# A Mamba and mixture-of-experts layer in a software pipeline: two groups of the D term as TensorE products with a diagonal, two C-weighted states through ScalarE and GpSimd, and the FFN's slots moved

## The reference, cut to what matters

```python
x = x + _layernorm(mamba(_layernorm(x)))
x = x + _layernorm(ffn(_layernorm(x)))
# mamba: 512 inner channels, 16 states, 4 taps
x_in, z = split(x @ W_in)
u = silu(causal_depthwise_conv(x_in) + conv_b)
dt_lr, B, C = split(u @ W_xproj)
delta = softplus(dt_lr @ W_dt + b_dt)
h_t = exp(delta_t * A) * h_(t-1) + (delta_t * u_t) * B_t      # for each of 16 states n
y_t = sum over n of C_t[n] * h_t[n]
y = (y + D_skip * u) * silu(z)                                # D_skip * u is the D term
out = y @ W_out
# ffn: shared silu(x@g)*(x@u)@d, and 8 experts weighted by the top 2 of softmax(x @ router)
```

## Time and profile before

| | before |
|---|---|
| time, median of 3 runs (range) | 2335.7 us (2333.97 to 2335.87) |
| the profiled execution's time | 2333.0 us |
| its span, first to last instruction | 2331.2 us |
| busy: DVE, PE, POOL, ACT | 2155.3, 2070.9, 1963.8, 1644.8 us |
| mean granted TensorE clock | 0.945 |

### The profile page before, as it was taken

The page is one execution under the profiler, slowest core; times in us unless marked ns, Lnnn a source line. Parts: engine busy times, 40 slices in busy tenths (PEclk is TensorE's granted clock), DMA queues, the critical chain, the costliest instruction groups (busy, mean ns, idle before and its releaser), DMA issues. The chain is left out here.

```text
span 2331.2 us, 30455 instructions
## 1 busy us (share of the span) xinstructions
PE 2070.9 (89%) x9280; PEld 1347.3 (58%) x9280; DVE 2155.3 (92%) x3056; ACT 1644.8 (71%) x2488; POOL 1963.8 (84%) x1625
## 2 busy tenths in 40 slices
PE   7678989999898999989899999998989989997978
PEld 4355665656566565655656566565656656565654
DVE  4999999999999999999999999999999999998950
ACT  5656877777777676777777777777768777775632
POOL 4677998989989898998989899898988989798844
PEclk8659999999999999999999999999999999998979
DMA  5111212211122121112211121121122111111201
GB/s 144 33 44 37 71 55 60 59 55 55 56 64 64 51 68 51 56 57 63 64 51 59 60 60 55 60 59 56 50 67 61 55 60 50 55 56 46 71 20 46
DMA packets 92995, 134.28 MB, mean 58 GB/s; under 512 B 12048, under 2 KB 43024, under 8 KB 92832
## 3 DMA queue, kind: packets, MB, share of 16 engines
q1 hardware_dynamic: 92832, 132.34, 18.4%
HBM read 123.13 MB, written 9.18 MB: 57 GB/s over the span
## 5 line engine op out<-in xcount | busy, mean ns | idle before, releaser
L836 DVE TENSOR_TENSOR_SCAN h<-d_a,carry,d_bu 128x512 f32<-128x512 f32 x1024 | 1261.1, 1267 | 47.0 <-ACT d_a L633 38.4
L1103 POOL TENSOR_TENSOR d_bu<-delta_u,b_rows 128x1024 f32<-128x1024 f32 x512 | 1202.2, 2359 | 4.4 <-issue 0.2
L633 ACT ACTIVATE d_a<-delta,a_neg 128x512 f32<-128x512 f32 x1024 | 699.6, 691 | 499.0 <-DVE h L836 493.9
L465 PE MATMUL ht<-ident,h 128*128 128x128 f32 x4096 | 607.3, 293 | 100.9 <-DVE y_t L846 94.3
L465 PEld LDWEIGHTS ht<-ident,h 128*128 128x128 f32 x4096 | 503.5, 150 | 333.6 <-issue 123.3
L846 DVE SCALAR_TENSOR_TENSOR y_t<-ht,c_t,y_t 128x512 f32<-128x512 f32 x896 | 621.5, 735 | 2.2 <-PE ht L465 1.5
L540 PE MATMUL ring<-x_t,w_gate_sb 128*128 128x512 f32 x640 | 327.8, 638 | 21.7 <-ACT delta L798 17.9
L567 PE MATMUL dn<-w_down_sb,up_hidden 128*128 128x256 f32 x1280 | 302.9, 379 | 1.7 <-POOL up_hidden L1166 1.7
L547 PE MATMUL ring<-x_t,w_up_sb 128*128 128x512 f32 x640 | 292.5, 600 | 11.9 <-ACT silu_gate L732 11.8
L1161 POOL TENSOR_TENSOR up_hidden<-silu_gate,up_hidden 128x512 f32<-128x512 f32 x160 | 204.3, 1277 | 110.8 <-ACT up_hidden L736 79.6
L567 PEld LDWEIGHTS dn<-w_down_sb,up_hidden 128*128 128x128 f32 x1280 | 236.0, 190 | 60.0 <-issue 31.8
(11 more groups left out here) (127 smaller groups left out, 2029.3 us busy)
## 6 DMA issues: line engine op xcount, KB each, us to landing
b_rows<-b_rows_hbm SPq DMA_DIRECT2D x256, 256.0 KB, 3.4
coef_rows<-coef_rows_hbm SPq DMA_DIRECT2D x128, 256.0 KB, 3.5
xa<-L_attn_x_in SPq DMA_DIRECT2D x16, 512.0 KB, 5.0
xr<-L_attn_x_in SPq DMA_DIRECT2D x16, 512.0 KB, 5.1
out<-xr SPq DMA_DIRECT2D x15, 512.0 KB, 2.9
w_in_sb<-L_attn_W_in_in SPq DMA_DIRECT2D x1, 1024.0 KB, 6.3
w_gate_sb<-L_ffn_experts_gate_in SPq DMA_DIRECT2D x2, 512.0 KB, 4.9
w_up_sb<-L_ffn_experts_up_in SPq DMA_DIRECT2D x2, 512.0 KB, 5.5
```

The lines of the kernel that those rows point to most:

```text
L465: last = nc.tensor.transpose(HT[q % HTS][:, j * P:(j + 1) * P], H[:, (NS * c + n) % HS, j, a * P:(a + 1) * P], IDN[:, :])
L633: nc.scalar.activation(DA[i % DAS][:, :], DL[:, r, j, :], ACT.Exp, scale=ANEG[:, j, n:n + 1]).then_inc(ex.sem, 1)
L836: nc.vector.tensor_tensor_scan(H[:, (NS * s + n) % HS, j, :], DA[(n * J + j) % DAS][:, :], BU[:, (2 * n + j // 2) % 4, j % 2, :], CARRY[:, ...
L1103: nc.gpsimd.tensor_tensor(BU[:, (2 * n + h) % 4, :, :], DU[:, 2 * h:2 * h + 2, :], BB[:, n % 2, :].unsqueeze(1).to_broadcast([P, 2, T]), A ...
```

## The change

1. **D term of groups 0 and 1.** Two 128x128 diagonals of D_skip (`DIAG`) are made once. At the end of slot 63 PE multiplies them with u (`skip_product`) into the ring banks, and `transpose_y` adds its transposes on top instead of starting the bank. DVE's `skip_u` of these groups becomes a plain copy by ACT in slot 3 (`copy_y`). Groups 2 and 3 stay on DVE in slot 5. Their transposes go from slot 4 to slot 3, ahead of `x_in` (0).
2. **Two pieces of y.** Pieces 14 and 15, which DVE added in slot 20, are written with their C by ACT in slot 20 into `UP` (`side_state`), and POOL adds both onto `y_t` in slot 22 (`side_sum`). DVE's next add on the same rows, piece 18 in slot 24, waits for it.
3. **Slots.** Pairs 1 to 4 come two slots earlier, both gates of pair 1 are in slot 20, delta comes two slots earlier, the statistics of xa are in slots 16, 16, 24, 24 (before: 16, 16, 26, 36) and its mean in 30 (42). `cf` and `ct` go to the dn banks, are copied in slot 20 itself, and `ct` comes from slot 48 to slot 20, ahead of the first down product.

```diff
-        yd, y_first, y_last, xt = stage("yd", J), stage("y_first", NT), stage("y_last", NT), stage("xt", KM)
+        yd_copy, diag = stage("yd_copy", 2), stage("diag", 0)
+        yd, y_first, y_last, xt = stage("yd", J - 2), stage("y_first", NT), stage("y_last", NT), stage("xt", KM)
...
-        YD_PE, YD_DVE, Y_GATE, OUT_PE = (1, 4), (3, 3, 5, 5), 4, (5, 5, 6, 6)
+        YD_PE, YD_ACT, YD_DVE, Y_GATE, OUT_PE = (1, 3), 3, {2: 5, 3: 5}, 4, (5, 5, 6, 6)
...
-        PAIR_AT = (12, 22, 32, 42, 50)
+        PAIR_AT = (12, 20, 30, 40, 48)
+        GATE_AT = (12, 13, 20, 20, 30, 31, 40, 41, 48, 49)
...
+                    if with_scan and t == SLOTS - 1:
+                        for j in range(2):
+                            skip_product(s, lo, r, j)
+
+            def skip_product(c, lo, r, j):
+
+                pe.wait_ge(diag.sem, 2)
+                pe.wait_ge(u_s.sem, u_s.at(c, j + 1))
+                pe.wait_ge(*ring_user_before(c + 1, lo + 1, "yd", j))
+                nc.tensor.matmul(yd_bank(j)[:, :], DIAG[:, j, :], U[:, r, j, :], start=True, stop=False,
+                                 skip_group_check=True)
...
                 pe.wait_ge(*added(s - 1, SLOTS - NT - 1))
-                if j < 2:
-                    pe.wait_ge(*ring_user_before(s, lo, "yd", j))
-                else:
+                if j >= 2:
                     pe.wait_ge(norm["y"].sem, norm["y"].at(s - 2))
+                    if exists(lo):
+                        pe.wait_ge(ct.sem, ct.at(s))
...
+            def side_state(c, r, q):
+
+                n, a = q // NT, q % NT
+                act.wait_ge(ht_full.sem, ht_full.at(c, q + 1))
+                act.wait_ge(hf.sem, hf.at(c - 1, up_used(1)))
+                act.wait_ge(y_sum.sem, y_sum.at(c - 1))
+                nc.scalar.activation(UP[:, q - SIDE_Q[0], :], HT[q % HTS][:, :], ACT.Copy,
+                                     scale=CT[:, r, a, n:n + 1]).then_inc(y_side.sem, 1)
...
+            def copy_y(c, j, prepared):
+
+                act.wait_ge(full["yd"].sem, full["yd"].at(c, j + 1))
+                act.wait_ge(conv_last.sem, conv_last.at(prepared))
+                act.wait_ge(o_full.sem, o_full.at(c - 1))
+                nc.scalar.activation(YD[:, j, :], yd_bank(j)[:, :], ACT.Copy).then_inc(yd_copy.sem, 1)
...
+            def side_sum(c):
+
+                a = SIDE_Q[0] % NT
+                pool.wait_ge(y_side.sem, y_side.at(c))
+                pool.wait_ge(*added(c, SIDE_Q[1] - NT))
+                nc.gpsimd.tensor_tensor(YT[:, a:a + 2, :], YT[:, a:a + 2, :],
+                                        UP[:, :, :], ALU.add).then_inc(y_sum.sem, 1)
```

More of the change, by code:

```diff
@@ L163, in mamba_moe_kernel @@
         shift = {w: stage(f"shift_{w}", n) for w, n in dict(xa=2, o=2, x1=2, y=2).items()}
+        y_side, y_sum = stage("y_side", 2), stage("y_sum", 1)
         stream, tail = stage("stream", 1), stage("tail", NT)
-        scan, add_c, carry = stage("scan", NS * J), stage("add_c", (NS - 2) * NT), stage("carry_s", NS)
+        scan, add_c, carry = stage("scan", NS * J), stage("add_c", (NS - 2) * NT - 2), stage("carry_s", NS)
         stats = {w: stage(f"stats_{w}_s", 2 * NT) for w in ("xa", "o", "x1", "y")}
@@ L217, in z_bank @@
             return DN[j] if j < 2 else ring_bank("z", j)
+        SIDE_Q = ADDS[SIDE_SLOT]
         def added(c, q):
@@ L553, in ffn_part @@
                     pe.wait_ge(rt.sem, rt.at(c))
-                    pe.wait_ge(*ring_user_before(s, lo, "cf", 0))
-                    bank = ring_bank("cf", 0)
+                    pe.wait_ge(x1t.sem, x1t.at(c))
+                    bank = DN[1]
                     for a in range(NT):
-                        last = nc.tensor.matmul(bank[0:E, a * P:(a + 1) * P], COEF[:, a, :],
-                                                IDN[:, :], start=True, stop=True)
+                        last = nc.tensor.transpose(bank[0:E, a * P:(a + 1) * P], COEF[:, a, :], IDN[:, :])
                     last.then_inc(full["cf"].sem, 1)
@@ L695, in body @@
                         first_state(s, r, t - NT - 1)
+                    if with_scan and t == SIDE_SLOT:
+                        for q in SIDE_Q:
+                            side_state(s, r, q)
                     if ffn and t == 1:
@@ L699, in body @@
                         normed_y(s - 2)
+                    if ffn and t == YD_ACT:
+                        for j in range(2):
+                            copy_y(s - 1, j, s if with_scan else s - 1)
                     if ffn:
@@ L803, in prep_part @@
                     nc.scalar.activation(CT[:, o, :, :].rearrange("p a n -> p (a n)"),
-                                         ring_bank("ct", 0)[:, 0:NT * NS], ACT.Copy).then_inc(ct.sem, 1)
+                                         CT_BANK, ACT.Copy).then_inc(ct.sem, 1)
             run(body)
@@ L826, in finish_constants @@
                 dve.wait_ge(consts.sem, 1)
+                for j in range(2):
+                    nc.vector.tensor_scalar(DIAG[:, j, :], IDN[:, :], DSK[:, j:j + 1], None, ALU.mult)\
+                      .then_inc(diag.sem, 1)
             def scan_step(s, r, n, j):
@@ L895, in body @@
                     for q in ADDS.get(t, ()):
-                        if with_scan and q >= NT:
+                        if with_scan and q >= NT and q not in SIDE_Q:
                             add_state(s, r, q)
@@ L958, in ffn_part @@
             def ffn_part(c, o, t, prepared):
-                for j in range(J):
+                for j in range(2, J):
                     if t == YD_DVE[j]:
@@ L1130, in body @@
                         rstd_of("xa", s + 2)
+                    if with_scan and t == SIDE_SLOT + 2:
+                        side_sum(s)
                     for f in range(F):
@@ L1150, in gate_y @@
             def gate_y(c, o, j):
-                pool.wait_ge(yd.sem, yd.at(c, j + 1))
+                if j < 2:
+                    pool.wait_ge(yd_copy.sem, yd_copy.at(c, j + 1))
+                else:
+                    pool.wait_ge(yd.sem, yd.at(c, j - 1))
                 pool.wait_ge(sz.sem, sz.at(c))
```

63 lines of the change are left out of this document (41 added, 22 removed).

## The result

| | before | after |
|---|---|---|
| time, median of 20 runs each (range), same chip | 2334.49 us (2332.19 to 2336.9) | 2338.58 us (2334.7 to 2340.06) |
| ratio to before, 95% interval | | 1.0016 [1.0010, 1.0023] |
| span of the profiled execution | 2331.2 us | 2337.3 us |
| mean granted TensorE clock | 0.945 | 0.963 |

The changed kernel is slower by 0.1 to 0.23%, some 4 us. The forecast was 2332, so faster by 0.16% than the 2335.7 us known then. The time lies in the forecast range; the sign is wrong.

The account below looks back on a forecast made before the run. DVE, busy 134.17 of a pass's 137.32 us, was taken as the bound. 15 x (-0.2) - 1.3 + 1 = -3.3 took 2333.0 to 2329.7 us, forecast as a median of 2332 us, range 2306 to 2350.

Parts of the forecast that it names:

- Removed from DVE: Per pass, 1.72 us of D-term evictions in slot 3 and 1.30 us of adds in slot 20, together 3.02 us.
- step (4): Head: DVE starts the statistics of out 0.4 us later, not 1.7 us earlier; the saving becomes 2.1 us of waits.
- Added elsewhere: Per pass: PE 124.93 becomes 126.7 us, ACT 103.18 becomes 105.7, POOL 123.04 becomes 125.4; none becomes the bound.
- steps (1) to (5): Head: piece 60 0.5 us late, then normed_y, PE's projection, DVE's statistics and ACT's later work, up to 1.1 us late.
- step (3): Head: dn transposes wait for normed_y with x_in (0) behind; PE's unbroken 13.04 us begins at 1143.1, ends 1.1 us later.
- Net at scan 12: End of the head's reckoning: scan 12 begins 0.5 us later than before, between 0 and +2.0 in other cases.
- Slots 20 to 27: DVE's 1.30 us of adds removed there; scan 25 at +0.3 us against before, scan 27 at -0.05 us.
- the rest of a pass: Silu and softplus blocks move two slots earlier; 0.15 us less by the pieces, making -0.2 us a pass in all.
- A: Head: PE catches up its 1.1 us before the statistics; passes 1.1 to 1.3 us shorter, 2314 us; chance 0.25.
- B: Slot 20: cf and C come late to ACT, delaying scan 25; +1.0 to +1.4 us a pass, 2350 us; chance 0.20.
- C: Slot 24: POOL's sum is late for DVE's piece 18; +1.3 us a pass, 2351 us; chance 0.05.
- D: ScalarE's new work much dearer than VectorE's, 2.2 us each; side states add 3.2 us, 2380 us; chance 0.02.

Follow-up runs that it names:

- e5: The changed kernel without the two products with the diagonal, so the D term of groups 0 and 1 is missing from the result: 2322.77 us, ratio 0.9955.
- e6: The changed kernel with the two products moved behind the last four pieces, ahead of the transposes of y: 2327.38 us, ratio 0.9972.
- e9: The changed kernel with the two products as last matmuls into the ring banks, where PE waits for normed_y: 2328.28 us, ratio 0.9972.
- e2: The changed kernel without the D term's change and its order; side states and new slots stay: 2321.06 us, ratio 0.9941.
- e7: The changed kernel with ACT's copies of y ahead of normed_y and the dn transposes behind x_in (0): 2334.05 us, ratio 0.9999.
- e4: The changed kernel plus fourteen unread transposes of the identity in PE's wait for normed_y: 2332.73 us, ratio 0.9994.
- e1: The changed kernel without side states and POOL's sum; DVE adds pieces 14 and 15 again: 2361.76 us, ratio 1.0118.
- e10: The changed kernel with each product with the diagonal issued twice in its place: 2373.82 us, ratio 1.0168.
- e8: The changed kernel with products behind the last pieces, ACT's copies of y ahead of normed_y and dn transposes behind x_in (0): 2346.46 us, ratio 1.0061.

## Why the prediction went wrong, step by step

**Removed from DVE (3.02 us a pass).** The part of it in the head, 1.72 us, is worth near nothing. DVE is busy for 132.32 us in a pass of 137.36 with the high clock (131.5 forecast), and idle for 5.04 instead of 3.15 (+2 forecast); the window view of the changed kernel, as the earlier trace rows:

```profile
994.60:1131.96 137.36, 124.66 (x573) 79.37 (x573) 132.32 (x187) 104.98 (x161) 125.55 (x103) 1.00 0.18 58
```

e5, e6 and e9 show the most that the 1.72 us of the D term can bring in the head: 25.68 against 25.94 before and 25.78 in e2, so 0.1 to 0.3 us. Slots 8 to 19 take 0.34 back; that belongs to the order of the dn transposes, `x_in` and ACT's copies, for e5 has it and e7 has not. Without any product at all (e5) the D term's change still gains nothing over e2 (2322.8 against 2321.1). That DVE's head saving turns into waits was step (4), and it holds.

**Added elsewhere: right.** Two side states took 1.25 us (1.29 forecast), two copies of y 1.11 (1.16), POOL's sum 2.36; the products with the clock high 1.79 from start to start (1137.35 - 1135.56), as forecast. The ACT rows of the changed kernel at slots 20 to 25:

```profile
1192.84 1.25 ACT L680 ACTIVATE up_hidden<-ht,c_t 128x512 f32<-128x512 f32 x2
1194.12 0.59 ACT L795 ACTIVATE x_dbl<-dn 8x512 f32<-8x512 f32 x1
1194.73 0.22 ACT L857 ACTIVATE c_t<-dn 128x64 f32<-128x64 f32 x1
...
1199.85 1.30 ACT L663 ACTIVATE d_a<-delta,a_neg 128x512 f32<-128x512 f32 x2
```

**The head, steps (1) to (5): right in the passes with the high clock, and the step that failed in the others is step (3).** PE's wait for `normed_y` was forecast at about 2 us and is 2.04; DVE waits 0.90 us at scan 5 and 0.34 at the statistics. Net at scan 12 I had +0.5 us. In a pass with the high clock scan 12 begins 1032.39 - 994.60 = 37.79 us behind slot 61's aggregate, before it was 1168.23 - 1130.96 = 37.27 (the earlier trace rows has scan 12 at 1167.01 + 1.22), so +0.52:

```profile
1032.39 1.28 DVE L893 TENSOR_TENSOR_SCAN h<-d_a,carry,d_bu 128x512 f32<-128x512 f32 x1 [0.23 <-ACT d_a L663]
```

Head and slots 8 to 19 together are 0.25 + 0.34 = +0.59 longer there. In six other passes they are 1.94 + 0.34 = +2.28. Step (3) priced the transposes and the products of `x_in` at the speed of the earlier trace rows, "PE's unbroken work of 13.04 us", and moved it by 1.1 us as if its length could not change. It is 1.7 us longer when the clock falls into it: 0.46 in the transposes, 1.27 in `x_in`.

What the clock is worth in the sum: over the thirteen passes the changed kernel loses 11.7 us to stretches longer than their shortest, 10.1 of them in those six heads and 1.3 in the head where the products were hit. The kernel before loses 5.3 us in the same way, 2.8 in its heads and 2.5 in slots 19 to 61. The window view from 840 to 1400 us has a fall of the clock in each such stretch. So 6.4 us come from falls that meet the path at dearer places than before, a term that the sum put at nothing. The forecast for thirteen passes was -2.6 us, the measurement +7.2: of these 9.8 us the clock makes 6.4. The other 3.4 us lie between the shortest passes, 137.36 against 137.31 where the forecast had -0.2 (see slots 20 to 27 below). The mean clock of the profile, 0.945, stood on the page before; I had left it out of the sum.

Why the fall meets this place is settled only in part. e5 shows that the wait alone does not bring it. e4 shows that filling the wait removes it there. All kernels here have falls somewhere, and the edits move them: behind the wait (after, e1), onto the products (e4, e7), onto the pieces (e5, e6, e9). What decides the place, the runs leave open; and the place is seen only in the one execution that was profiled (two of the 20 runs of the changed kernel took 2334.7 and 2334.9 us, and why is not known). The Trainium skill (TensorE: Matmul & The Clock Gate, Part 1) says that the clock follows how busy the engine has lately been, and that the window over which this is judged is free-running and does not start anew with the kernel. A fall that comes in turn with the passes, and moves with the edits, is compatible with that; no run here shows the window itself.

**Slots 20 to 27: right; the rest of a pass 0.2 us too hopeful.** Behind scan 12 I had +0.5 going down to -0.2, so -0.7 us. Between the shortest passes it goes from +0.52 to +0.05, so -0.47. (Slots 19 to 61 alone measure -0.53 there and -9.1 / 13 = -0.70 in the mean, but the mean holds the falls in the kernel before.) Scan 20 to scan 25 shrank from 9.83 us to 9.68, with a wait for the decay (0.42; 0.3 forecast), and scan 20 to scan 27 from 13.83 to 13.36, so -0.47 (-0.55 forecast). That is all that is gained behind scan 12; of the 0.15 us that I had counted in the rest of a pass nothing is seen. In fifteen passes the two make some 3 us. DVE, the changed kernel:

```profile
1190.90 3.63 DVE L893 TENSOR_TENSOR_SCAN h<-d_a,carry,d_bu 128x512 f32<-128x512 f32 x3
...
1200.58 2.46 DVE L893 TENSOR_TENSOR_SCAN h<-d_a,carry,d_bu 128x512 f32<-128x512 f32 x2 [0.42 <-ACT d_a L663]
...
1204.26 2.45 DVE L893 TENSOR_TENSOR_SCAN h<-d_a,carry,d_bu 128x512 f32<-128x512 f32 x2
```

**Rivals.** A did not come: PE does not catch up its lateness before the statistics. B and C did not either: ACT goes from the side states straight to cf and C, and POOL starts its sum at once and ends at 1196.5, with no wait of DVE for it. D is excluded by the durations: the copies take 0.63 us each and the side states 0.67, not 2.2. None of the rivals had the clock, though the range held the time.

**The version that beats both.** e2 keeps the side states and the slots and leaves the D term on DVE: 2321.06 us, 0.6% less than before, 17.5 us less than the changed kernel. Its shortest passes are 136.6 us long (before 137.31).

## What to carry to other kernels

Before work is taken off the busiest engine, ask at the next place where two engines meet which of them comes last there: in this head it was TensorE by 0.1 to 0.3 us, so 1.7 us less on DVE could bring no more, while 1.8 us more on TensorE ahead of the last pieces cost 0.5 us a pass, and another 1.8 us (e10) went into it one for one. The same matmuls cost nothing in the head behind those pieces while the clock was high: place added work in the engine's wait, not ahead of what others wait for. A profile with a mean clock under 1 has slow stretches somewhere; look where they lie, and give a change that moves idle time on TensorE a term for them meeting the critical stretch.

## What was not expected of the hardware

- TensorE's granted clock falls to its lower level in a kernel that keeps the engine busy for 88% of the span, for some 3 to 7 us at a time (the windows over the head of the changed kernel and over e9's pieces), in a pattern of its own: in the head of every second pass (changed kernel), of every pass (e1), or with three lengths of the head in turn (e8: 27.06, 28.2 and 28.7 us). It cost 0.7 us on the last pieces (e5), 0.9 to 1.3 with the products (e4, e7) and 1.7 on the transposes and `x_in`.
- Work without any use made the kernel faster: 1.7 us of idle transposes a pass, 2338.6 to 2332.7 us.
- A higher mean clock did not go with a shorter time: 0.963 at 2338.6 us against 0.945 at 2334.5. What counts is where it is low.
